# Layer 1 of a two-layer transformer on one core: output products of the last batch split by chunk, their sums kept in SBUF, first feed-forward weights loaded by themselves, former output products moved one place later

## The reference

```
q, k, v = split(cond(x) @ w_attn + b_attn)    # cond: conditioning scan; heads of width 32
att = softmax(where(causal, q k^T * scale, -inf))
y = (att @ v), heads joined
x = x + y @ w_proj + b_proj                  # attention output, here called x3
z = cond2(x)                                 # bidirectional scan over the sequence, and sigmoid(x)
D = gelu(float16(z) @ W0.T + bias0), float16
x = x + float16(D @ W1.T + bias1)            # what the program returns
```

## Time and profile before

| | us |
|---|---|
| three runs | 2153.51, 2153.31, 2149.83 (median 2153.31) |
| profiled execution, its own time | 2150.08 |
| span of the profile | 2148.4 |
| TensorE matmul busy | 1905.7 (89% of the span) |
| VectorE, ScalarE, GpSimd busy | 1603.8, 1362.4, 1130.4 |
| mean granted TensorE clock | 0.957 of full speed |

### The profile page before, as it was taken

One profiled execution on the slowest core, in us unless ns is written; L12 is line 12 of the kernel. 1 busy time (PEld: TensorE's weight loads), 2 busy tenths in 40 slices (PEclk: granted clock), 3 DMA queues, 4 the chain that ended last, 5 costly groups with the idle time before them and its releaser, 6 DMA issues. The chain is left out here.

```text
span 2148.4 us, 40251 instructions
## 1 busy us (share of the span) xinstructions
PE 1905.7 (89%) x14509; PEld 1186.3 (55%) x14509; DVE 1603.8 (75%) x3518; ACT 1362.4 (63%) x3320; POOL 1130.4 (53%) x877
## 2 busy tenths in 40 slices
PE   0789999999999999999996799777898989878999
PEld 0455566566666666666665465445666666633444
DVE  7799988888888887888763599657778687834760
ACT  6587777777767767777753244256867676835442
POOL 5687786776776776666640489543323132200440
PEclk9899999999999999999997899978999999989999
DMA  5333331322213212343215844374434243345100
GB/s 179 123 114 128 114 108 56 117 70 70 84 65 94 75 69 75 113 138 109 82 52 189 338 155 146 136 256 152 130 114 134 92 136 126 111 145 179 40 20 20
DMA packets 106861, 249.88 MB, mean 116 GB/s; under 512 B 10480, under 2 KB 39280, under 8 KB 104624
## 3 DMA queue, kind: packets, MB, share of 16 engines
q1 hardware_dynamic: 83872, 190.49, 26.5%
q10 hardware_dynamic: 19680, 46.67, 6.3%
q0 software_dynamic: 3120, 10.23, 1.6%
HBM read 175.26 MB, written 68.94 MB: 114 GB/s over the span
## 5 line engine op out<-in xcount | busy, mean ns | idle before, releaser
L996 PE MATMUL ps_q<-a_y,a_w 128*128 128x512 f16 x1536 | 343.8, 381 | 58.3 <-POOL a_y L691 57.7
L996 PEld LDWEIGHTS ps_q<-a_y,a_w 128*128 128x128 f16 x1536 | 147.6, 98 | 226.3 <-issue 60.9
L714 POOL TENSOR_TENSOR a_rb<-a_rb,router_y 128x512 f32<-128x512 f32 x128 | 181.8, 1420 | 167.2 <-ACT a_rb L857 166.4
L1210 DVE TENSOR_REDUCE a_nmax<-ps_s 128x1 f32<-128x512 f32 (+3 forms) x256 | 123.8, 484 | 111.2 <-PE ps_s L1017 111.1
L1005 PE MATMUL ps_v<-a_w,a_y 128*128 128x128 f16 x3072 | 182.9, 220 | 0.0
L856 ACT ACTIVATE a_rb<-ps_q 64x512 f32<-64x512 f32 x128 | 76.0, 593 | 168.7 <-DVE a_ra L1195 167.1
L1043 PE MATMUL ps_o<-a_tt_,a_v 128*128 128x512 f32 (+3 forms) x512 | 157.0, 451 | 25.5 <-ACT a_tt_ L899 22.2
L1005 PEld LDWEIGHTS ps_v<-a_w,a_y 128*128 128x128 f16 x3072 | 175.2, 98 | 1.2
L1065 PE MATMUL ps_v<-a_o,a_wo 128*128 128x512 f16 x732 | 168.0, 379 | 1.9 <-ACT a_v L883 1.9
L876 ACT ACTIVATE ps_s<-ps_s,a_nmax 128x512 f32<-128x512 f32 (+3 forms) x256 | 125.1, 489 | 39.8 <-DVE a_nmax L1212 39.7
L2211 ACT ACTIVATE a_ef<-ps,a_nmax 128x512 f32<-128x512 f32 (+3 forms) x256 | 131.7, 535 | 26.6 <-DVE a_nmax L2575 25.1
(11 more groups left out here) (344 smaller groups left out, 4977.6 us busy)
## 6 DMA issues: line engine op xcount, KB each, us to landing
a_w<-wqkv_split SPq DMA_DIRECT2D x48, 768.0 KB, 4.5
scratch_numlog<-wkv_nl ACTq DMA_DIRECT2D x40, 512.0 KB, 2.8
wkv_kt<-in_fT ACTq DMA_DIRECT2D x56, 256.0 KB, 2.7
router_y<-in_wqkv SPq DMA_DIRECT2D x16, 768.0 KB, 5.4
wqkv_split<-a_w SPq DMA_DIRECT2D x16, 768.0 KB, 6.9
a_stacks<-qk_parts SPq DMA_DIRECT2D x96, 128.0 KB, 2.6
gate_up<-in_gate_up SPq DMA_DIRECT2D x8, 1408.0 KB, 17.5
a_nlc<-scratch_numlog SPq DMA_DIRECT2D x17, 512.0 KB, 5.1
```

The source lines that it names most:

```text
L714: pool.tensor_tensor(rb[:, n, :], rb[:, n, :], rot[:, 2 * n + 1, :], ALU.mult).then_inc(s["roped"], 1)
L996: mm = pe.matmul(psq[n][:], w16[:, g % 2, wp, n, c, :], y16[b % 2][:, yp, c, :], start=c + m == 0, stop=c == CC - 1 and m == 2)
L1210: dve.tensor_reduce(nmax[:, 0, j:j + 1], cols(ps, j), AX, ALU.max, negate=True)
```

## The change

Four things are changed in layer 1:

1. The output products of batches 0 to 2, made in the next batch at q = 0, i = 3, stand one place later on TensorE and VectorE: `output(0)` behind the scores, `output(1)` behind `turn`, `output(2)` behind `values`, `output(3)` at the end as before.
2. The output products of the last batch are split by chunk (`output_heads(co, bank, lo, hi)`). Chunks 0 to 2, nine matmuls per product, are made ahead of `values` of head 63 (products 0 to 2) and behind it (product 3), and chunk 3, three matmuls per product, after `turn_output`. Each product has a bank of its own, the three of `ps[0]` and the first of `ps[1]`.
3. The last batch's x3 isn't stored. The tile x3 is allocated ahead of both parts (`early.x3`), and the feed-forward part reads batch 3 from it in place of loading it. For its room, the eight exponentials are written into `stage`, after the last low half of the weights has been made (`lo` at 8).
4. In the feed-forward part SyncE issues weight piece 2, and so everything behind it, only when piece 1 has landed.

```diff
--- before.py
+++ after.py
@@ -139,7 +139,7 @@
 
 
 
-    def __init__(self, k, ctx, name, tiles, slots, raws=1, apart=None, scans=None, decays=None, front=None):
+    def __init__(self, k, ctx, name, tiles, slots, raws=1, apart=None, scans=None, decays=None, front=None, ek_raw=None):
         nc = k.nc
         self.k, self.tiles, self.raws, self.apart = k, tiles, raws, apart
         self.decays = None if decays is None else decays.rearrange("p (b n) -> p b n", b=B)
@@ -149,7 +149,7 @@
             return ctx.enter_context(nc.sbuf_tensor(f"{name}_{n}", s, F32))
 
         self.kt = [sb(f"kt{i}", [P, T]) for i in range(tiles)]
-        self.ek_raw = [sb(f"ek_raw{i}", [P, T]) for i in range(raws)]
+        self.ek_raw = ek_raw or [sb(f"ek_raw{i}", [P, T]) for i in range(raws)]
         self.ek, self.ekv = sb("ek", [P, T]), sb("ekv", [P, T])
         self.euk, self.eukv = sb("euk", [P, T]), sb("eukv", [P, T])
         self.fwd, self.bwd = scans or (sb("fwd", [P, 2, T]), sb("bwd", [P, 2, T]))
@@ -1833,6 +1833,7 @@
 
     def __init__(self, k, ctx):
         self.k = k
+        self.x3 = ctx.enter_context(k.nc.sbuf_tensor("ff_x3", [P, CC, T], F32, side="right"))
         room = ctx.enter_context(k.nc.sbuf_tensor("ff_room", [P, 2 * TT * C], F32, side="right"))
         self.got = room[:].rearrange("p (n c) -> p n c", c=C)
         n = CC * T // 2
@@ -1887,7 +1888,7 @@
         t16 = sb("t16", [P, 2, 2, 3, 512], F16)
         ob = sb("ob", [P, 2, TT, P])
         ot16 = sb("ot16", [P, 2, CC, T], F16)
-        x3 = sb("x3", [P, CC, T])
+        x3 = early.x3
         ps = [[ctx.enter_context(nc.psum_tensor(f"ps1_{a}{i}", [P, 512], F32)) for i in range(3)] for a in range(2)]
         pso = ctx.enter_context(nc.psum_tensor("ps1_o", [P, 512], F32))
         psp = ctx.enter_context(nc.psum_tensor("ps1_p", [P, 512], F32))
@@ -1945,8 +1946,9 @@
         def final(b):
             return isinstance(b, int) and b == B - 1
 
-        def out_bank(co):
-            return pso if co % 2 else psp
+        def last_bank(co):
+
+            return (*ps[0], ps[1][0])[co]
 
         def bank_of(i):
             return ps[1][i % 2] if i < 2 * TT else pso
@@ -2059,10 +2061,7 @@
                 with sp.Fori(1, B - 1) as b:
                     batch(b, False)
                 batch(B - 1, False)
-                for co in range(CC):
-                    sp.wait_ge(s["x3"], (B - 1) * CC + co + 1)
-                    sp.dma_start(d["x3"][B - 1, co], x3[:, co]).then_inc(s["x3_stored"], 16)
-                sp.wait_ge(s["x3_stored"], 16 * (B - 1 + CC))
+                sp.wait_ge(s["x3_stored"], 16 * (B - 1))
                 sp.wait_ge(s["stacked"], B * CC * 16 * 6)
 
             @block.gpsimd
@@ -2437,12 +2436,16 @@
                         mm = pe.transpose(psp[:, t * P:(t + 1) * P], ob[:, q % 2, t, :], k.ident[:])
                     mm.then_inc(s["ot_ps"], 1)
 
-                def output(co, bank=psp):
-                    for c in range(CC):
+                def output_heads(co, bank, lo, hi):
+                    for c in range(lo, hi):
                         for n, (op, wpart) in enumerate(PARTS):
                             mm = pe.matmul(bank[:], wp16[:, wpart, c, co * P:(co + 1) * P], ot16[:, op, c, :],
                                            start=c + n == 0, stop=c == CC - 1 and n == 2)
-                    mm.then_inc(s["proj"], 1)
+                    if hi == CC:
+                        mm.then_inc(s["proj"], 1)
+
+                def output(co):
+                    output_heads(co, psp, 0, CC)
 
 
                 for i in range(TT):
@@ -2468,11 +2471,6 @@
 
                             more = not final(b) or q + 1 < CC
                             last_output = i == 3 and q == 0 and not first
-                            if last_output:
-                                pe.wait_ge(s["wp_lo"], CC)
-                                pe.wait_ge(s["vf"], it + 2)
-                                output(0)
-
                             if first and h == 0:
                                 pe.wait_ge(s["x2"], 2 * TT)
                             if i < HPC - 1:
@@ -2492,16 +2490,20 @@
                                     pe.wait_ge(s["vf"], it + 1)
                                 turn_output(it - 1, q + 1)
                             if last_output:
+                                pe.wait_ge(s["wp_lo"], CC)
+                                pe.wait_ge(s["vf"], it + 2)
+                                output(0)
+                            turn(h, i)
+                            if last_output:
                                 pe.wait_ge(s["x3"], (b - 1) * CC + 1)
                                 output(1)
-                            turn(h, i)
-                            if last_output:
-                                pe.wait_ge(s["x3"], (b - 1) * CC + 2)
-                                output(2)
                             if i == 1:
                                 pe.wait_ge(s["vlo"], it + 1)
                             if i or q or not first:
                                 values(h - 1, q if i else q + 1, (i - 1) % HPC)
+                            if last_output:
+                                pe.wait_ge(s["x3"], (b - 1) * CC + 2)
+                                output(2)
                             if i == 0 and more:
                                 if q == CC - 1:
                                     pe.wait_ge(s["y_here"], b * 16 + 32)
@@ -2529,15 +2531,17 @@
                 with pe.Fori(1, B - 1) as b:
                     batch(b, False)
                 batch(B - 1, False)
+                pe.wait_ge(s["wp_lo"], CC)
+                pe.wait_ge(s["ot_lo"], B * CC - 1)
+                for co in range(CC - 1):
+                    output_heads(co, last_bank(co), 0, CC - 1)
                 pe.wait_ge(s["tlo"], B * H1 * 3)
                 values(B * H1 - 1, CC - 1, HPC - 1)
-                pe.wait_ge(s["ot_lo"], B * CC - 1)
+                output_heads(CC - 1, last_bank(CC - 1), 0, CC - 1)
                 turn_output(B * CC - 1, CC - 1)
                 pe.wait_ge(s["ot_lo"], B * CC)
                 for co in range(CC):
-                    if co >= 2:
-                        pe.wait_ge(s["x3"], (B - 1) * CC + co - 1)
-                    output(co, out_bank(co))
+                    output_heads(co, last_bank(co), CC - 1, CC)
 
             @block.vector
             def _(dve):
@@ -2657,8 +2661,6 @@
                         for i in range(HPC):
                             h = b * H1 + (q * HPC + i)
                             last_output = i == 3 and q == 0 and not first
-                            if last_output:
-                                output(b - 1, 0)
                             if i == 1 and (q or not first):
                                 ot_low(it - 1, (q - 1) % CC)
                             if first and 0 < h <= 2 * TT:
@@ -2669,12 +2671,14 @@
                             if more or i + 1 < HPC:
                                 maxima(h + 1, i + 1)
                             if last_output:
-                                output(b - 1, 1)
+                                output(b - 1, 0)
                             turned_low(h, i)
                             if last_output:
-                                output(b - 1, 2)
+                                output(b - 1, 1)
                             if i or q or not first:
                                 out(h - 1, q if i else q + 1, (i - 1) % HPC)
+                            if last_output:
+                                output(b - 1, 2)
                             late = first and q == 0
                             if final(b) and i == 1:
                                 dve.wait_ge(s["f_sig"], q + 1)
@@ -2712,7 +2716,7 @@
                 out(B * H1 - 1, CC - 1, HPC - 1)
                 ot_low(B * CC - 1, CC - 1)
                 for co in range(CC):
-                    output(B - 1, co, out_bank(co))
+                    output(B - 1, co, last_bank(co))
 
 
 def layer1_ffn(k, w, early):
@@ -2750,7 +2754,8 @@
         LAYER = 3
         FIRST = 2
         UNITS = (B - FIRST) * CC
-        wkv = Wkv(k, ctx, "wkvf", UNITS, 0, raws=UNITS, apart=nl, scans=scans)
+        wkv = Wkv(k, ctx, "wkvf", UNITS, 0, raws=UNITS, apart=nl, scans=scans,
+                  ek_raw=[stage[:, u // CC, u % CC * T:(u % CC + 1) * T] for u in range(UNITS)])
 
         def unit(u):
             return FIRST + u // CC, u % CC * LAYERS + LAYER
@@ -2766,7 +2771,8 @@
             return w0_rest[:, part, i - 1] if i else early.w0[:, part]
 
         def batch_x(b):
-            return xt[:, bass.ds(b % 2, 1)].rearrange("p a c n -> p (a c) n")
+
+            return early.x3 if b == B - 1 else xt[:, b % 2]
 
         with nc.Block() as block:
 
@@ -2774,6 +2780,8 @@
             def _(sp):
                 def raw(i):
                     src = d["w0"][:, :, i * HN:(i + 1) * HN] if i < NQ else d["w1"][:, :, (i - NQ) * CN:(i - NQ + 1) * CN]
```

(11 more changed lines are left out.)

## The result

The changed kernel takes 2135.52 us (median of 4 runs, 2133.41 to 2138.44) against 2152.14 us for the kernel before (4 runs, 2149.83 to 2153.51): a ratio of 0.9927, with a 95% interval of 0.9912 to 0.9943, or 16.6 us less. The forecast was 2137.5 with a range of 2131 to 2145.

What follows compares the result with a forecast made beforehand. The chain of waits ends in the feed-forward part, with TensorE fully busy from 1960.8 to 2143.0. 5.2 + 8.1 + 0.9 = 14.2 us off 2150.08 gave 2135.9, taken as 2137.5 for the runs' higher median; range 2131 to 2145.

Steps and rivals of the forecast that it cites:

- Part 1: At q = 0, i = 3 of batches 1 to 3, later output products save 0.9, 2.6 and 1.7 us, together 5.2.
- The new wait ahead of `output(3)`: At q = 0, i = 3, nothing is left to hide VectorE's addition behind, so TensorE waits 1.0 us.
- With most of it filled I take the drop as gone: In batch 2, filling the 2.32 us of idle time removes the 1.2 GHz stretch, worth 1.7 us.
- The rival that part 1 gives nothing: At q = 0, i = 3, waits eat the gain and batch 2's low clock stays or moves: 2142.7 us, chance 0.12.
- Part 2: At the end of the attention, split products and the dropped store start the feed-forward 8.1 us earlier.
- the end at low clock throughout: Rival: all products at the attention's end run at low clock, 0.9 us worse there, 2146.5 us in all, chance 0.05.
- Part 3: At the feed-forward's start, loading the first weights alone gains 1.4 us, of which 0.9 stays.
- Piece 1 lands at 7.2: Before the change, the weight piece lands 7.2 us after the first issue; held alone, at 5.7 to 6.0.
- the first rival: At the feed-forward's start, later weights pay for the first ones, costing 1.5 us: 2139.9 us, chance 0.14.
- so it doesn't get in the way: In the feed-forward, the first quarter ends at 10.2 us, before the second quarter's start at 10.4.
- Nothing behind 1960.8: TensorE is busy from 1960.8 to 2143.0 us, so the removed x3 load of batch 3 there counts at 0.
- Slower: Rival: the clock stays low over the denser stretches in attention and feed-forward, 2161.2 us, chance 0.02.

Runs made afterwards that it cites:

- the early outputs: The changed kernel with ScalarE's first two feed-forward outputs of batch 0 moved ahead of the eight exponentials: 2129.35 us, ratio 0.9887 to the kernel before.
- the places alone: The kernel before with only the output products of batches 0 to 2 moved one place later on TensorE and VectorE: 2146.93 us, ratio 0.9967.

## Why the prediction was right

**Part 1 (5.2 us).** Place by place the first profile gives 1.0, 2.7 and 1.7, where the text had 0.9, 2.6 and 1.7. The new wait ahead of `output(3)` was put at 1.0 and measures 0.79: 0.69 for the addition and 0.10 of signalling, where the text had 0.15 on either side. The exactness is partly luck. "With most of it filled I take the drop as gone" failed as a rule: with the idle time filled, six of seven profiles still had the place in batch 2 at 18.0 to 18.1, with a stretch at 1.2 GHz, and three of them another place as well. The average over all profiles is 4.7; timing gives 7.1 (0.9967; 2.8 to 11.2 us by its interval), too wide to tell the two apart. The rival that part 1 gives nothing is out, since the interval lies below 1.

**Part 2 (8.1 us).** Measured 9.5 in the profile and 8.7 on average. The chain went step by step as written: 27 matmuls, `values`, nine matmuls, `turn_output`, the halves, four additions, then the next block. Two sizes were off. The clock was back after 0.9 us of the split products rather than 2.85 (6.33 us from 1878.92 to the next `values`, against 7.25), and 0.3 us, not 0.4, is the blocks' change. The early rise is luck in part: over the eight split profiles the clock was back 1 to 3 us after the first split product, and the 27 matmuls took 6.3 to 7.3 us. ScalarE's own store, put at 1896.0 just ahead of VectorE's 1896.9, did not become the end. In the words of the rivals, no profile had the end at low clock throughout.

**Part 3 (0.9 us).** The net was 0 instead, and the step that failed is its first number: "Piece 1 lands at 7.2" was taken for what the unheld issue costs, but seven of eight profiles have 5.8 to 6.3. The second quarter's start after the change, forecast at 10.4, measured 10.43. The third quarter did not wait for piece 2, which landed in 5.5 us, not 7.2 to 8.1: the first rival is out too. In the first comparison the second quarter did come 1.4 us earlier, and what ate that was not on the list. The text let the first quarter end at 10.2 "so it doesn't get in the way"; it ended at 7.35 (1894.03 + 7.08, less 1893.76), TensorE idled 3.09 us in its place, and the second quarter paid 1.5 us at 1.2 GHz.

**Nothing behind 1960.8.** The dropped load of x3 was counted at 0. From the output products to the end the kernels with it take 208.8 to 210.4 us, those without it and without the early outputs 208.7 to 210.6. The exponentials' new wait cost nothing that shows: TensorE idles 8.09 us there after, 8.82 before.

**Slower** had 0.02 for a clock that stays low over denser work. It rose within 1 to 3 us in every split end profiled.

**The sum.** 14.2 forecast, 16.6 measured by the medians. The parts measured alone come to 0.33%, 0.41% and 0.05%, 0.79% or 17 us together, against 0.73% for the whole. The stretches give less, some 4.7 + 8.7 - 1.3 = 12.1 us (1.3 for the output products, 32.9 us behind the first weight on average without the store and 31.6 with it), or 14.9 if the one profile of each kernel is taken. The difference is no larger than the wander of the stretches that no edit touches, 90.0 to 97.4 us for those between the places, but what makes it up isn't shown.

## What to carry to other kernels

Where a product over chunks waits for its last chunk in a serial tail, give each product its own bank and do the finished chunks ahead of the wait: it fills idle time and shortens what is left to a quarter. Look next at each in-order engine for a short instruction that frees a bank but stands behind a transfer; here moving two was worth 6 to 9 us, about as much as the whole tail (8.7). A size that is read from one profile, such as a landing time, should be read from several before a term is made of it.

## What had not been expected of the hardware

- A first quarter that ran faster brought nothing. In all six kernels in which it started behind 1.30 us of idle time and piece 1 was whole, it ran at 2.4 GHz, and the idle time of 3.1 to 3.6 us behind it was followed by a stretch at 1.2 GHz that cost about 1.5 us; one profile with 3.41 us of idle time had none. The Trainium skill (TensorE: Matmul & The Clock Gate, "HAM oscillation — how this bites in real kernels") describes this kind of alternation between a wait for a transfer and a slow restart. The rows 1.00 and 0.51 above agree; the profile with 3.41 us of idle time doesn't.
- A stretch at 1.2 GHz can lie across dense work: 1693.5 to 1697.1 in the kernel with the places alone, with one gap of 0.44 us in the 5 us before it.
- Identical code ahead of the change reached the attention of layer 1 anywhere from 1397.2 to 1406.1 us, more than half the whole effect.
- A half piece (512 KB), with its other half issued right behind it, landed in 4.8 us and a whole one (1 MB) in 5.8: half the bytes took away 1.0 us, not half the time.
